# A feed-forward of sixteen batches as seven block products instead of eight, in two passes over its hidden width

## The reference

```
x  = query + attention(...)                       # stage A of the kernel
h  = layer_norm(x, ln2_g, ln2_b)
ff = gelu(h @ w1 + b1, approximate=False) @ w2 + b2   # w1: 512x2048, w2: 2048x512
out = x + ff
```

## Time and profile before

| what | value |
|---|---|
| median of 3 runs | 3094.44 us (3094.41 to 3095.11) |
| the profiled execution: its time, its span | 3096.19 us, 3094.5 us |
| busy over the span: PE, PEld, DVE, ACT, POOL | 96%, 78%, 49%, 37%, 15% |
| mean granted TensorE clock | 0.982 |
| stage B | from about 1587 us to the end of the span |
| HBM traffic: read, written | 97.02 MB, 33.55 MB |

### The profile page before, as it was taken

One profiled execution on the slowest core, in us unless ns is written; L12 is line 12 of the kernel. 1 busy time (PEld: TensorE's weight loads), 2 busy tenths in 40 slices (PEclk: granted clock), 3 DMA queues, 4 the chain that ended last, 5 costly groups with the idle time before them and its releaser, 6 DMA issues. The chain is left out here.

```text
span 3094.5 us, 52560 instructions
## 1 busy us (share of the span) xinstructions
PE 2965.2 (96%) x17576; PEld 2408.6 (78%) x17576; DVE 1520.4 (49%) x4100; ACT 1153.1 (37%) x2958; POOL 459.1 (15%) x432
## 2 busy tenths in 40 slices
PE   6999999999999999999979999999999999999999
PEld 5777877778777777777758888888888888888887
DVE  4766666666676666766634333322333322333322
ACT  3655566555666565655622111111111111111111
POOL 1222122211222112222112000000000000000000
PEclk9999999999999999999979999999999999999999
DMA  5766676666666666666522111100111100111100
GB/s 133 122 113 102 111 107 111 115 110 108 107 108 119 112 102 115 103 119 110 89 85 82 41 41 41 41 9 32 41 41 41 41 31 10 41 41 41 41 27 14
DMA packets 123695, 231.89 MB, mean 75 GB/s; under 512 B 10752, under 2 KB 10752, under 8 KB 123648
## 3 DMA queue, kind: packets, MB, share of 16 engines
q1 hardware_dynamic: 123648, 231.28, 37.5%
HBM read 97.02 MB, written 33.55 MB: 42 GB/s over the span
## 5 line engine op out<-in xcount | busy, mean ns | idle before, releaser
L710 ACT ACTIVATE sm<-sm,mins 128x128 f32<-128x128 f32 (+3 forms) x1024 | 571.7, 559 | 606.4 <-DVE mins L574 603.6
L574 DVE CUSTOM_DVE_ANT_0 sm<-bank_s,mask 128x128 f32<-128x128 f32 (+3 forms) x1024 | 480.7, 488 | 451.2 <-PE bank_s L425 440.5
L1146 ACT ACTIVATE g_sb<-bank_f,b1s 128x512 f32<-128x512 f32 x256 | 176.2, 688 | 1173.1 <-PE bank_f L956 1173.1
L1058 DVE CAST g_hi<-g_sb 128x512 fp32r<-128x512 f32 x256 | 113.0, 441 | 866.9 <-ACT g_sb L1146 866.9
L437 PE MATMUL bank_t<-ident,sm 128*128 128x128 f32 x2560 | 424.1, 281 | 53.5 <-ACT pT L520 34.1
L437 PEld LDWEIGHTS bank_t<-ident,sm 128*128 128x128 f32 x2560 | 305.8, 143 | 156.9 <-issue 76.6
L954 PE MATMUL bank_f<-hT_hi,w_hi 128*128 128x512 f32 x1024 | 407.6, 398 | 1.6 <-DVE hT_lo L1052 1.6
L954 PE MATMUL bank_o<-w_hi,g_hi 128*128 128x512 f32 x1024 | 408.0, 398 | 0.0
L956 PE MATMUL bank_f<-hT_hi,w_lo 128*128 128x512 f32 x1024 | 406.7, 397 | 0.0
L955 PE MATMUL bank_f<-hT_lo,w_hi 128*128 128x512 f32 x1024 | 406.4, 397 | 0.0
L956 PE MATMUL bank_o<-w_hi,g_lo 128*128 128x512 f32 x1024 | 406.3, 397 | 0.0
(11 more groups left out here) (108 smaller groups left out, 4486.5 us busy)
## 6 DMA issues: line engine op xcount, KB each, us to landing
stack<-st_hi SPq DMA_DIRECT2D x256, 256.0 KB, 5.6
xt<-in_x SPq DMA_DIRECT2D x32, 1024.0 KB, 5.3
stack<-st_lo SPq DMA_DIRECT2D x128, 256.0 KB, 7.2
c_raw<-in_ctxT SPq DMA_DIRECT2D x64, 256.0 KB, 6.0
x_scratch<-xt SPq DMA_DIRECT2D x64, 256.0 KB, 2.0
xn<-x_scratch SPq DMA_DIRECT2D x16, 1024.0 KB, 7.7
xr<-x_scratch SPq DMA_DIRECT2D x16, 1024.0 KB, 5.6
out<-xr SPq DMA_DIRECT2D x64, 256.0 KB, 2.1
```

The source lines that it names most:

```text
L574: op = V.tensor_tensor_reduce(sm[:, n % SLOTS_S, off:off + w], bank_s[n % BANKS_S][:, off:off + w], mask[:, 512 - w:512], 1.0, 0.0, ALU.ad ...
L710: op = A.activation(row, row, ACT.Exp, bias=mins[:, g % 2, c:c + 1], scale=-1.0, accum_out=sums[:, g % 2, c:c + 1])
L1058: V.tensor_copy(g_hi[:, f % RING_H, :], g_sb[:, f % 2, :]).then_inc(g_hi_ok, 1)
L1146: A.activation(g_sb[:, f % 2, :], bank_f[f % 2][:], ACT.Gelu, bias=b1s[:, f:f + 1], scale=1.0).then_inc(gelu, 1)
```

## The change

In pass `ph` (0 or 1) the kernel does one half of F, 1024 wide, for all 16 batches. Pass 0 stores x + b2 + its half of the output back into `x1`, and pass 1 adds the other half and stores `out`.

Within a pass both layers are done in blocks of 2x2 (Strassen in Winograd's form). Each 2x2 block product is made of seven products of blocks instead of eight. Layer 1 does this twice (`d` = 0, 1, each 512 of F): the operands are A11, A12, S1 to S4, A22 of the weights and B11, B21, B22, T1 to T4 of h, and `layer1` is one of the seven products: 12 matmuls of 256 columns. Layer 2 is done once over 1024: `layer2` is one of seven products of 24 matmuls of 256 columns, in two halves. For one batch and pass that is 14 x 12 + 7 x 24 = 336 matmuls of 256 columns.

The sums and differences that this needs are put on VectorE: of the weights (`w1_parts`, `w2_parts`, once for each part and pass), of h (`h_parts`, T1 to T4, pass 0 only), of the results of layer 1 (`add`), of the gelu's outputs (`a_sum`), of the output (`sum_out`), and all low halves (`low`). ScalarE makes all high halves, the gelu in pieces of 256 columns, copies of three results out of PSUM, and it applies the norm's gain and offset to h (`x_high`) so that `scale_w1` and `bias_product` are gone. GpSimd keeps the power and the addition of b2 (pass 0 only).

The seven operands of h in halves (`b_hi`, `b_lo`, 14,336 bytes for each partition and half, 3.67 MB in all) are stored to `b_scratch` in DRAM in pass 0 and loaded again in pass 1. There is one copy of each in SBUF.

The core of the diff (the lists below are new too):

```diff
+    STEPS = [(0, 0), (0, 1), (0, 2), (0, 3), (0, 4), (0, 5), (1, 0), (0, 6),
+             (1, 1), (1, 2), (1, 3), (1, 4), (1, 5), (1, 6)]
+    X_AFTER = {8: 0, 9: 1, 10: 2, 11: 3}
...
+            def layer1(c, ph, first, d, at_place):
...
+                if d == 0 and ph == 1 and at_place == 0:
+                    pe.wait_ge(b_in, (c - B) * 32 + 32)
...
+                if at_place == 5:
+                    pe.wait_ge(copied, at(c, COPIES, (d, "U2")))
+                if at_place == 6:
+                    pe.wait_ge(added, at(c, ADDS, (d, "C22")))
...
+            def layer2(c, ph, first, k):
...
+                if k == 4:
+                    pe.wait_ge(summed, at(c, OUTPUTS, 2))
...
+                if k == 6:
+                    pe.wait_ge(summed, at(c, OUTPUTS, 4))
+                for h in range(2):
...
+                    pe.wait_ge(a_lo_ok, at(c, A_LOW, (k, h)))
...
+            def body(c, ph, first, last):
+                for n, (d, place) in enumerate(STEPS):
+                    if n == 13:
+                        layer2(c, ph, first, 0)
+                    layer1(c, ph, first, d, place)
+                    if n in X_AFTER and ph == 0 and not last:
+                        x_transpose(c + 1, X_AFTER[n], bank_t)
+                for k in range(1, 7):
+                    layer2(c, ph, first, k)
```

VectorE's order for one batch and pass, which the prediction walks through (`norm` is true in pass 0 except for the last batch; `w1_parts` and `w2_parts` stand in it in the first and last batch of pass 0 and in the first of pass 1):

```diff
+            def body(c, ph, first, last):
+                norm = ph == 0 and not last
+                if ph == 0:
+                    h_parts(c, 4)
...
+                if norm:
+                    for t in range(QT):
+                        layer_norm_stats(c + 1, t)
+                add(c, 0, "C11")
+                if norm:
+                    normalise(c + 1, 0)
+                    normalise(c + 1, 1)
+                add(c, 0, "C12")
+                a_low(c, 0, 0)
+                if norm:
+                    normalise(c + 1, 2)
+                    normalise(c + 1, 3)
+                add(c, 0, "C22")
+                a_sum(c, "S1", 0)
+                a_low(c, 1, 0)
+                a_sum(c, "S2", 0)
...
+                add(c, 1, "C11")
+                add(c, 1, "C12")
+                a_low(c, 0, 1)
+                add(c, 1, "C22")
+                a_sum(c, "S1", 1)
+                a_low(c, 1, 1)
+                a_sum(c, "S2", 1)
+                sum_out(c, ph, 0)
+                a_low(c, 2, 0)
+                a_low(c, 2, 1)
+                if norm:
+                    h_parts(c + 1, 0)
+                a_sum(c, "S4", 0)
+                a_low(c, 3, 0)
+                a_sum(c, "S4", 1)
+                a_low(c, 3, 1)
+                sum_out(c, ph, 1)
+                if norm:
+                    h_parts(c + 1, 1)
+                a_sum(c, "S3", 0)
+                a_sum(c, "S3", 1)
+                a_low(c, 4, 0)
+                sum_out(c, ph, 2)
+                a_low(c, 4, 1)
+                if norm:
+                    h_parts(c + 1, 2)
+                a_low(c, 5, 0)
+                sum_out(c, ph, 3)
+                a_low(c, 5, 1)
+                if norm:
+                    h_parts(c + 1, 3)
+                a_low(c, 6, 0)
+                sum_out(c, ph, 4)
+                a_low(c, 6, 1)
...
+                sum_out(c, ph, 5)
+                sum_out(c, ph, 6)
```

`h_parts(m, stage)` is 3, 2, 2, 2 and 2 instructions for the stages 0 to 4 (low B11, sums T1 and T3; lows T1, B21; low B22, sum T2; low T2, sum T4; lows T3, T4). ScalarE's end of a batch, and SP's loads of pass 1:

```diff
+                a_high(c, 4, 0)
+                a_high(c, 4, 1)
+                if norm:
+                    h_high(c + 1, "T2")
+                a_high(c, 5, 0)
+                a_high(c, 5, 1)
+                if norm:
+                    h_high(c + 1, "T4")
+                a_high(c, 6, 0)
...
+                if ph == 1 and not last or ph == 0 and last:
+                    sp.wait_ge(step1, at(c, STEPS, (1, 6)))
+                    sp.wait_ge(b_stored, 32 * B)
+                    for part, m in enumerate((b_hi, b_lo)):
+                        sp.dma_start(m[:].rearrange("p a k s -> p (a k s)").bitcast(F32),
+                                     b_view(0 if ph == 0 else b + 1, part)).then_inc(b_in, 16)
```

More of the change, by code:

```diff
@@ L837, in _, with stage_b @@
             over_batches(pool, body)
-def stage_b(nc, x1, w1, w2, vecs, b2, out):
+def stage_b(nc, x1, b_scratch, w1, w2, vecs, b2, out):
     B, S, D = x1.shape
@@ new lines, in stage_b, with at, before @@
+        step1, copied, added, gelu = (sem(n) for n in ("step1", "copied", "added", "gelu"))
+        a_hi_ok, a_sum_ok, a_lo_ok = (sem(n) for n in ("a_hi_ok", "a_sum_ok", "a_lo_ok"))
+        step2, summed, xr_ok = (sem(n) for n in ("step2", "summed", "xr_ok"))
+        def at(c, table, what):
+            return c * len(table) + (len(table) + table.index(what) + 1)
+        def before(c, table, what):
+            return c * len(table) + (table.index(what) + 1)
+        HALVES = [(k, h) for k in range(7) for h in range(2)]
@@ L937, in body @@
[L937 to L945, removed]
@@ L950, in _ @@
+            body(0, 0, True, False, ahead=True)
+            with sp.Fori(1, B - 2) as c:
+                body(c, 0, False, False, ahead=True)
+            body(B - 2, 0, False, False)
+            body(B - 1, 0, False, True)
+            body(B, 1, True, False)
+            with sp.Fori(B + 1, 2 * B - 1) as c:
+                body(c, 1, False, False)
+            body(2 * B - 1, 1, False, True)
+            sp.wait_ge(stored, 64 * B + 32)
         @block.tensor
         def _(pe):
[L952 to L963, removed]
-                mm.then_inc(x_t, 1)
[L966 to L986, removed]
@@ L1000, in _ @@
[L1000 to L1024, removed]
@@ new lines, in activate @@
+            def activate(c, ph, d, name):
+                rows = "C1 C2".split().index(name[:2])
+                if name == "C21":
+                    act.wait_ge(step1, at(c, STEPS, (d, 6)))
+                else:
+                    act.wait_ge(added, at(c, ADDS, (d, name)))
+                for m in range(2):
+                    to = g_block(d, name)[:, m, :]
+                    f = 2 * KT + 8 * ph + 4 * rows + 2 * d + m
+                    op = A.activation(to, bank_x[d][:, C * m:C * m + C] if name == "C21" else to, ACT.Gelu,
+                                      bias=vec[:, f:f + 1], scale=1.0)
+                op.then_inc(gelu, 1)
@@ new lines, in a_high @@
+            def a_high(c, k, h):
+                if k < 2:
+                    act.wait_ge(step2, before(c, HALVES, (6 - k, h)))
+                else:
+                    act.wait_ge(step2, at(c, HALVES, (k - 2, h)))
+                if k in (0, 3, 6):
+                    act.wait_ge(gelu, at(c, GELUS, (h, {0: "C11", 3: "C21", 6: "C22"}[k])))
+                else:
+                    act.wait_ge(a_sum_ok, at(c, A_SUMS, ({1: "S1", 2: "S2", 4: "S3", 5: "S4"}[k], h)))
+                A.copy(a_part(a_hi, k, h), a_source(k, h)).then_inc(a_hi_ok, 1)
```

588 lines of the change are left out of this document (424 added, 164 removed).

## The result

The changed kernel is slower: 3139.24 us median (3136.69 to 3142.42) against 3094.78, a ratio of 1.0143 (95% interval 1.0126 to 1.0161). The prediction was 3088 with a range to 3130, so it is 51 us low and the time lies outside the range. It had 6 us less than before, and the change costs 44 us more; its chances were even, 0.41 for faster and 0.42 for slower. The profiled execution has a span of 3135.9 us.

The account below looks back on a forecast made before the run. TensorE's issue was taken as the bound. Batch 0 ends at 1692, 14 batches of 48.7 reach 2374, the seam's 111 reaches 2485, 15 of 39.8 reach 3082, tail 4.5 and some 2 give 3088 us; range 3025 to 3130.

Parts of the forecast that it names:

- 7.5 + 17 + 6.7: Seam between passes: TensorE's delays in us from the new weights' parts, on top of 47.3 + 39.8, for 111 us.
- I take 118.3 ns, the mean over the 18: TensorE's price for a 256-column matmul, from stage A's short runs, range 117.1 to 119.1 ns; 39.8 us a batch and pass.
- two times 0.87: TensorE's 16 transposes in a batch of pass 0, taken as 1.7 us, making 41.5 us with the products.
- some 2 for starts at the low clock: Term at the end of the sum: about 2 us for starts at the low clock, beside a tail of 4.5.
- Sum 6.0: TensorE's stalls from VectorE's order in a batch of pass 0: 6.0 us together, making the period 47.5 before GpSimd's additions.
- I take 1.2: Pass 0: GpSimd's additions of b2 meeting VectorE cost 1.2 us a batch (0 to 2.2), making 48.7.
- 11 x 0.61 + 2 x 0.5 = 7.7 us: Time of one weight part: 11 VectorE operations, with each sum's high half on ScalarE in between, 7.7 us.
- The clock's rival: Pass 0: low clock after the gap before layer2(6) costs 1.9 us a batch, +27, 3115 us; chance 0.22.
- The reload: Pass 1: h's operands return by DMA in time, nothing added; rival has them 2 to 5 us late, 3140; chance 0.08.
- Dearer meetings and seams: Rival: GpSimd's additions cost 2.2 and weight parts a third more, +14 and +15, 3117 us; chance 0.10.
- VectorE keeps up: Rival: only half of the order's stalls come in pass 0, 45 less, 3043 us, or none, 2990; chance 0.20.
- three signs of being wrong: Pass 1 not clean, clock row below 0.95 in pass 0, or slack in VectorE's order where the walk stacked stalls.

Follow-up runs that it names:

- e6: e4 plus three first-half moves: norm's aggregation and normalisations later, x_high before a gelu, b2 additions behind the second transpose; 3025.6 us, ratio 0.9771.
- e7: Changed kernel without pass 1's loads of h's operands from DRAM; 3143.7 us, ratio 1.0147 to the kernel before.
- e1: Changed kernel without loading and preparing the second half's weights, so pass 1 reuses the first half's; 3098.5 us, ratio 1.0004 to the kernel before.
- e2: Changed kernel without GpSimd's four additions of b2 in pass 0; 3120.1 us, ratio 1.0074 to the kernel before.
- e3: Changed kernel without VectorE's sums and low halves of h for batches 1 to 15; 3051.0 us, ratio 0.9850 to the kernel before.
- e4: Changed kernel, all work kept, second half of the batch reordered on VectorE and ScalarE, layer 2 before h; 3056.7 us, ratio 0.9869 to the kernel before.
- e11: Changed kernel with e6's three first-half moves but without e4's order; 3106.6 us, ratio 1.0033 to the kernel before.
- e8: e6 with the second half's weight parts loaded in turn into two buffers instead of one; 3014.0 us, ratio 0.9734 to the kernel before.
- e9: e4 with only GpSimd's additions of b2 moved behind the second transpose; 3041.5 us, ratio 0.9820 to the kernel before.
- e10: e4 with only x_high of feature tile 1 moved ahead of the gelu of C11 on ScalarE; 3043.3 us, ratio 0.9824 to the kernel before.
- e5: Changed kernel with unread matmuls ahead of the waits before layer2(4), (5) and (6) in pass 0; 3132.8 us, ratio 1.0125 to the kernel before.

## Why the prediction was wrong

VectorE's queue was walked rightly, and the waits came out at nearly the sum forecast. Two terms of TensorE's own time failed, and each is half of the miss: the price of its instructions, and the time that it spends at the low clock. The profiled execution is 48 us over the forecast. First by stretch:

| stretch | forecast | measured | difference |
|---|---|---|---|
| end of batch 0 | 1692 | 1701.7 | +10 |
| 14 batches of pass 0 | 48.7 each | 50.0 each | +18 |
| seam, two batches | 111 | 126.1 | +15 |
| 15 batches of pass 1 | 39.8 each | 40.3 each | +8 |
| tail and starts at the low clock | 4.5 + 2 | 3.8 | -3 |

Then by cause. The share of the low clock is an estimate, worked out below. The forecast waits of batch 0 are its 79 us less 41.5, those of the seam 7.5 + 17 + 6.7:

| term | forecast | measured | difference |
|---|---|---|---|
| TensorE at the full clock: a batch of pass 0, of pass 1 | 41.5, 39.8 | 42.5, 40.3 | +24 |
| the low clock | 2 | some 26 | +24 |
| waits of the 14 batches: order and additions | 14 x 7.2 | 14 x 6.9 | -4 |
| first product and waits of batch 0 | 1613, 37.5 | 1615.6, 32.9 | -2 |
| waits of the seam | 31 | 38.0 | +7 |
| tail | 4.5 | 3.8 | -1 |

*TensorE's instructions.* The step that failed is "I take 118.3 ns, the mean over the 18", with the transposes at "two times 0.87". In pass 1 the window of 620 us has 5169 matmuls, 120.0 ns each, and 40.32 us a batch is 336 of them; the short runs of stage A had 117.1 to 119.1, so the whole range lay below. In pass 0 the transposes come on top with 2.2 us instead of 1.7 (42.5 less 40.3, e6). That is 1.0 us in each of 15 batches with transposes and 0.5 in each of the other 17. e7 excludes the reload as the cause. In pass 1 the weight loads' row is busy for all of the 620 us, which it was not before, so the loads may be what sets 120.0; that was not tested, and the cause stays open.

*The clock.* The sum has "some 2 for starts at the low clock" and nothing else; the rest of the clock stood among the rivals, and there only for pass 0. In batch 0 and in the seam TensorE is busy for longer than its products take at the full clock, at a mean granted clock of 0.78 and 0.82:

```profile
1616.00:1702.00 86.00, 53.09 (x357) 51.78 (x357) 60.24 (x100) 40.32 (x73) 6.50 (x5) 0.78 0.26 98
```
```profile
2401.80:2527.90 126.10, 88.12 (x674) 87.58 (x673) 76.82 (x117) 52.95 (x100) 6.39 (x4) 0.82 0.39 146
```

That is 53.1 us for the work of 42.5, and 88.1 for that of 80.6. With 5 of the 14 batches of pass 0 at 1.5 each it makes 10.6 + 7.5 + 7.6, some 26. For the seam e1 bears it out: with the weights' parts gone, and with them the waits of 10.8, 20.3 and 6.9 us, the clock is 1.00 there:

```profile
2418.00:2499.00 81.00, 80.55 (x672) 80.34 (x671) 47.14 (x73) 36.93 (x72) 5.96 (x4) 1.00 0.49 189
```

*Pass 0's waits.* The stall before `layer2(4)` came where it was forecast, 2.35 us in every batch for 2.4. Before `layer2(5)` TensorE waited in 4 batches of 14, 0.5 us, and before `layer2(6)` 1.1 to 1.9 us: it ran at the low clock in between, which took up the rest. As a whole they cost what was forecast. A batch of e2 without a costly fall of the clock takes 48.55 us, 6.0 above 42.5, and "Sum 6.0" was the forecast; e3, e4 and e11 show that VectorE's order is the cause. The additions of b2, "I take 1.2", cost 0.9 (e2): they started 10.6 us into the batch and not at 8.7, met S1 and S2, and delayed the third transpose by 0.4 to 1.4 us.

*The ends.* "11 x 0.61 + 2 x 0.5 = 7.7 us" for a part of the weights on VectorE is 8.4 (2450.7 to 2459.1), with a pause for ScalarE at two of the sums (0.69 before a low half). From the end of w1's second part, the chain of store, load of x and w2, and high half took 13.6 us to w2's part (2459.1 to 2472.7), where I had 9.7 (51.3 to 61). e1 shows that nothing else stands in the seam, and e8 that 12 us of it were one buffer used in sequence.

*The rivals.* The clock's rival had the right mechanism in its place before `layer2(6)`, but there it came in 3 batches of 14, and the clock cost more where no rival looked, in batch 0 and in the seam. The reload was hidden, as forecast: 1792 KB each, landed 7.5 and 11.2 us after issue, and e7 without it is no faster. "Dearer meetings and seams" had 0.10 and a price of 3117. It was half right: the meetings were cheaper than the sum's own 1.2, and the waits of the seam a fifth dearer. In "VectorE keeps up" half of the order's 6.0 is 14 x 3.0 and not 14 x 3.2, which changes little. None of the three signs of being wrong appeared (pass 1 is clean, the clock of pass 0 is 0.96, VectorE's order had little slack), because none of them looked at a matmul's price or at the clock outside pass 0. That the waits fit within 1 us in sum is partly luck: the additions and batch 0 came out below and the seam above.

*What the prediction missed most* is not in its sum. The period of pass 0 was read as given by the order that stands there, which is right, but the same walk says what another order costs: 3026 us with no instruction less (e6), and 3014 with a second buffer at the seam (e8).

## What to carry to other kernels

When an engine at 65% of its time makes the bound engine wait, walk its queue in order with the measured start-to-start distance; that walk was right to 1.2 us in 37 here, and it names the instructions to move. Work for the next batch belongs behind the work that the current one waits for, on the helper engine and on the one that feeds it (here ScalarE's high halves), and two moves against the same wait do not add in full (1.4 us a batch each in e9 and e10; with the third move 2.6 in e6). Take the bound engine's price per instruction from a long dense run, or put the error of a short one into the range: 1.7 ns in 118 became some 18 us here. Where the engine waits, ask at which clock it goes on. Price one-off preparation (weights at a start and a seam) like steady work: 8.4 us for a part on VectorE, and 45 us for those of the seam (e1).

## What the runs showed of the hardware

- GpSimd's additions and VectorE's instructions with two SBUF operands slowed each other: 1.78 us for the sum S2 instead of 0.69, and 6.41 for four additions that took 5.05 in e6. There they started 14.9 us into the batch instead of 10.6 and cost nothing.
- The granted clock fell to the lower of its two levels behind gaps of 2.4 us in otherwise dense work (0.60 over 2142 to 2146, the matmuls 0.21 us apart instead of 0.12). Filling the gaps with matmuls that nobody reads kept it at 1.00 (e5), and the distance from the awaited sum to the batch's last stayed 12.59 us: behind a wait for another engine, a low clock can cost nothing.
- A float32r matmul of 256 columns with a weight load of its own costs 120.0 ns in a dense stream, against 233.5 for 512 columns: 3% more for each column.
